# A gated attention block with a routed feed-forward part on one core: attention starts ahead of routing, normalized rows stay on chip, and value products are taken in plain fp32

## The reference

```python
# attn, per sequence (T=512, H=128, E=256, S=128)
xn2 = (xn - mean) / sqrt(var + EPS) * ln_w + ln_b
u, v, base = split(silu(xn2 @ uv_w.T + uv_b))
q, k = rope(base * gamma + beta)                 # two heads of one base
kernel = square(relu(q @ k.T / sqrt(S) + w[distance]))
attn = (u * (kernel @ v)) @ o_w.T + o_b + xn
# ffn, over all 4096 rows (8 experts, the best 2 of each row)
p = sigmoid(xn @ W_router); two largest, divided by their sum + 1e-6
ffn = sqrelu(xn @ W_sh_up) @ W_sh_down
    + sum over the two experts: weight * sqrelu(xn @ W_up[e]) @ W_down[e]
```

## Time and profile before

| | |
|---|---|
| median of 3 runs (lowest, highest) | 455.02 us (454.96, 456.42) |
| the profiled execution: its own time | 456.13 us |
| its span, first to last instruction | 454.3 us |
| PE busy | 371.5 us (82%), 2041 instructions |
| DVE busy | 294.0 us (65%), 726 |
| ACT busy | 245.2 us (54%), 453 |
| POOL busy | 176.2 us (39%), 159 |
| HBM read and written | 17.63 and 15.87 MB |
| mean granted TensorE clock | 0.927 of full |

### The profile page before, as it was taken

The page is one execution under the profiler, slowest core; times in us unless marked ns, Lnnn a source line. Parts: engine busy times, 40 slices in busy tenths (PEclk is TensorE's granted clock), DMA queues, the critical chain, the costliest instruction groups (busy, mean ns, idle before and its releaser), DMA issues.

```text
span 454.3 us, 8228 instructions
## 1 busy us (share of the span) xinstructions
PE 371.5 (82%) x2041; PEld 299.2 (66%) x2042; DVE 294.0 (65%) x726; ACT 245.2 (54%) x453; POOL 176.2 (39%) x159
## 2 busy tenths in 40 slices
PE   1168457799998989899999969999999999999800
PEld 1157435566665667566756638999999999999700
DVE  2889798988988888989899822333333333333245
ACT  0203027565676766665656715666666666666400
POOL 0486004562534526180716200444444444444500
PEclk9995567999999999999999997999999999999955
DMA  8618993000000001010100101221222212212089
GB/s 227 212 46 237 231 191 61 29 30 19 23 23 18 29 6 41 0 47 0 41 6 30 42 0 30 66 63 60 64 59 63 64 57 65 64 57 65 36 251 309
DMA packets 49792, 33.65 MB, mean 74 GB/s; under 512 B 5747, under 2 KB 46195, under 8 KB 49780
## 3 DMA queue, kind: packets, MB, share of 16 engines
q1 hardware_dynamic: 29120, 16.27, 12.8%
q10 hardware_dynamic: 16308, 8.26, 9.1%
q0 software_dynamic: 4352, 8.99, 5.5%
HBM read 17.63 MB, written 15.87 MB: 74 GB/s over the span
## 4 chain that ended last, share of the span: by engine, by line
PE 50%; DVE 21%; issue 12%; ACT 6%; ACTq 4%; DMA 4%; DVEq 2%; POOL 0%; POOLq 0%
PE bank L1133 14%; PE bank L1114 7%; PE bank L908 7%; PE bank L909 6%; PE bank L910 6%; DVE work L748 3%; PE bank L1020 3%; ACT base_qk L414 3%; DVE xs L613 3%; ACTq L356 2%; PE bank L946 2%; PE bank L1107 2%; DMA work<-results 2%; DVE qk_lo L725 2%; DVE k_lo L757 2%
## 5 line engine op out<-in xcount | busy, mean ns | idle before, releaser
L865 POOL DMA_INDIRECT slots_in<-xs,slot_now x64 | 75.2, 1176 | 124.5 <-DVE xs L634 77.9
L895 POOL DMA_INDIRECT results<-work x72 | 69.2, 960 | 109.2 <-DVE work L822 107.4
L822 DVE TENSOR_SCALAR work<-bank,work 128x128 f32<-128x128 f32 x72 | 25.2, 350 | 93.5 <-PE bank L1133 93.5
L1133 PEld LDWEIGHTS bank<-wdn,work 128*128 128x128 f32 x576 | 75.1, 191 | 6.0
L1133 PE MATMUL bank<-wdn,work 128*128 x576 | 75.7, 274 | 0.0
L499 ACT ACTIVATE work<-bank 128x512 f32<-128x512 f32 x72 | 43.1, 599 | 14.7 <-PE bank L1114 14.7
L505 ACT ACTIVATE work<-bank 128x512 f32<-128x512 f32 x72 | 43.1, 598 | 8.9 <-PE bank L910 3.4
L1114 PE MATMUL bank<-cst,work 128*128 128x128 f32 x288 | 43.9, 276 | 0.0
L908 PE MATMUL bank<-wup_lo,x_hi 128*128 x72 | 35.3, 491 | 1.0 <-DVE x_lo L813 1.0
L493 ACT CAST x_hi<-bank 128x128 fp32r<-128x128 f32 x72 | 19.0, 266 | 30.8 <-PE bank L1107 30.8
L1114 PEld LDWEIGHTS bank<-cst,work 128*128 128x128 f32 x288 | 34.2, 143 | 0.5 <-issue 0.4
(11 more groups left out here) (177 smaller groups left out, 824.1 us busy)
## 6 DMA issues: line engine op xcount, KB each, us to landing
slots_in<-spare ACTq DMA_DIRECT2D x1, 4680.0 KB, 31.7
work<-slots_in SPq DMA_DIRECT2D x36, 130.0 KB, 2.2
x_all<-in_L_attn_x SPq DMA_DIRECT2D x4, 512.0 KB, 8.7
work<-in_L_ffn_W_up SPq DMA_DIRECT2D x4, 512.0 KB, 3.5
wdn<-in_L_ffn_W_down SPq DMA_DIRECT2D x4, 512.0 KB, 7.3
work<-results SPq DMA_DIRECT2D x8, 256.0 KB, 7.2
work<-results ACTq DMA_DIRECT2D x8, 256.0 KB, 7.7
out<-x_all SPq DMA_DIRECT2D x8, 256.0 KB, 5.7
```

The costliest lines, as they stand in the source:

```text
L865: pool.indirect_dma_start(slots_in, bass.IndirectOffsetOnAxis(slot_now[:, k, t:t + 1], 0), xs1[:, k, t, :], None).then_inc(tokens_sent, 16)
L895: pool.indirect_dma_start(results, bass.IndirectOffsetOnAxis(dest[:, at:at + 1], 0), slot_y[:, k, :], None).then_inc(returned[k], 16)
L1133: last = pe.matmul(P_Y[h][:, 0:D], hid_t[:, h, rows], wdn[:, of, c, :].rearrange("p a d -> p (a d)"), start=(c == 0), stop=(c == HC - 1))
```

## The change

- The `Fori` loop over blocks is written out. Block 0 begins before routing; routing is cut in pieces that stand in blocks 0, 1 and 2.
- `x` comes in pieces of 4, 8, 10 and 10 tiles. Statistics and roots are taken for tiles 0 to 3 first, then for the other 28; the second norm's inverse is worked out on DVE (one more reciprocal), and both roots are asked for at once.
- `first_norm` writes normalized rows to `xs1` for all 32 tiles (132 wide: columns for a slot's address and weight on either side of the row). Groups 2 to 7 are made in block 0, and routing reads these same rows, turned by PE and copied by ACT. `second_norm` reads `xs1`.
- Each half row (130 of 132 columns, from column 0 or 2) is sent from `xs1` after the last routing piece; all 64 sends are one run on POOL. In the experts DVE adds the two column pairs of a slot row, since the pair that wasn't sent is zero.
- v and the squares are kept once, in fp32. `kernel_hi`, `kernel_lo`, `v_split` and one of two v silus are gone; `values` calls two plain matmuls instead of two `product`s.
- Weight casts go one expert at a time: in blocks 0 to 2 on ACT, their low halves and `add_rows` alternately on POOL. Down weights load after `routed`, since routing's scratch lies in their tile. The columns of gamma and beta, the cosines, the distance row and the zero fill move from ACT's queue to SP's.

The core of the diff (left out: names of semaphores, places of tiles, unchanged lines):

```diff
@@ sequence_turns @@
-            turn(0, True, False)
-            with eng.Fori(1, B - 1) as b:
-                turn(b, False, False)
-            turn(B - 1, False, True)
+            for b in range(B):
+                turn(b, b == 0, b == B - 1, b)
@@ ACT, turn @@
                 shared_square(b, 1)
+                if route == 0:
+                    routing_copied(2)
+                    routing_copied(3)
+                    routing_copied(4)
+                    routing_copied(5)
                 if not first:
                     output_out(b - 1)
-                kernel_hi(b, 0)
-                kernel_hi(b, 1)
+                if route == 1:
+                    weights_hi(3)
+                if route == 2:
+                    weights_hi(6)
                 shared_relu(b, 2)
                 shared_relu(b, 3)
+                if route == 0:
+                    routing_copied(6)
+                    routing_copied(7)
                 if not last:
                     second_rows_hi(b + 1)
                 shared_square(b, 2)
                 shared_square(b, 3)
-                kernel_hi(b, 2)
-                kernel_hi(b, 3)
+                if route == 0:
+                    weights_hi(1)
+                    weights_hi(2)
+                    routing_probs()
+                if route == 1:
+                    weights_hi(4)
+                    weights_hi(5)
+                if route == 2:
+                    weights_hi(7)
+                    weights_hi(8)
@@ DVE, routing's counts and statistics @@
+            def routing_counts():
+                dve.wait_ge(counted, 1)
+                dve.tensor_copy(place.rearrange(flat), banks[7][:, 0:NT * NE])
+                link(route_chain, dve.tensor_copy(sums[:, 0, 16:, :].rearrange(flat), banks[7][:, NT * NE:2 * NT * NE]))
+                dve.sem_inc(counts_kept, 1)
+                for n in range(5):
+                    src, dst, by = sums[:, n % 2], sums[:, (n + 1) % 2], 1 << n
...
+                link(stat_chain, dve.reciprocal(per_var[:, tiles], inv1[:, tiles]))
+                link(stat_chain, dve.tensor_tensor(inv2[:, tiles], var, per_var[:, tiles], ALU.mult))
+                dve.tensor_scalar(inv2[:, tiles], inv2[:, tiles], EPS, None, ALU.add).then_inc(var_made, 1)
@@ DVE, turn @@
                 qk_split(b)
+                if route == 0:
+                    first_norm(2)
+                    first_norm(3)
+                if route == 1:
+                    routing_first()
                 kernel_square(b, 0)
                 kernel_square(b, 1)
-                v_split(b)
+                if route == 0:
+                    first_norm(4)
+                    first_norm(5)
                 if not last:
                     second_norm(b + 1)
-                kernel_lo(b, 0)
-                kernel_lo(b, 1)
+                if route == 1:
+                    routing_second()
+                if route == 2:
+                    routing_counts()
                 kernel_square(b, 2)
                 kernel_square(b, 3)
+                if route == 0:
+                    first_norm(6)
+                    first_norm(7)
                 if not last:
                     second_rows_lo(b + 1)
-                    first_norm(b + 1)
+                if route == 1:
+                    routing_weights()
+                if route == 2:
+                    routing_tiles()
                 if not first:
                     mix(b - 1)
-                kernel_lo(b, 2)
-                kernel_lo(b, 3)
+                if route == 2:
+                    routing_slots()
                 if not last:
                     rotate_base(b + 1)
                     first_rows_lo(b + 1)
+                if route == 2:
+                    routing_owners()
@@ DVE, ahead of block 0 (the seven weight copies stand before this) @@
+            dve.wait_ge(inv_made, 1)
+            first_norm(0)
+            second_norm(0, True)
+            statistics(slice(FIRST, NT), ((1, (FIRST, 12)), (2, (12, 22)), (3, (22, NT))))
+            second_rows_lo(0)
...
+            dve.wait_ge(inv_made, 3)
+            first_norm(1)
             dve.wait_ge(ld["cos_sin"], 16)
-            first_norm(0, True)
             rotate_base(0)
             first_rows_lo(0)
@@ POOL @@
             pool.wait_ge(var_made, 1)
+            root(slice(0, 2), slice(0, FIRST))
+            pool.wait_ge(var_made, 2)
+            root(0, slice(FIRST, NT))
+            root(1, slice(FIRST, NT))
+            weights_lo(0)
+            for b in range(B):
+                add_rows(b)
+                weights_lo(b + 1)
+
+            pool.wait_ge(zero_filled, 16)
+            pool.wait_ge(slots_made, 1)
+            pool.sem_inc(sending, 1)
+            for t in range(NT):
                 for k in range(TOPK):
-                    pool.indirect_dma_start(slots_in, bass.IndirectOffsetOnAxis(slot_now[:, k, t:t + 1], 0),
-                                            xs1[:, k, t, :], None).then_inc(tokens_sent, 16)
+                    at = slice(k * 2, k * 2 + SENT_W)
+                    pool.indirect_dma_start(slots_in, bass.IndirectOffsetOnAxis(slot_i[:, k, t:t + 1], 0),
+                                            xs1[:, t, at], None, element_offset=k * 2).then_inc(tokens_sent, 16)
@@ PE, values and turn @@
-                    last = product(P_AV[e][:, :], v_hi[:, j, e * P:(e + 1) * P], v_lo[:, j, e * P:(e + 1) * P],
-                                   k_hi[:, j % 2, :], k_lo[:, j % 2, :], start=(j == 0), stop=(j == TB - 1))
+                    last = pe.matmul(P_AV[e][:, :], v[:, j, e * P:(e + 1) * P], kern[:, j, :], start=(j == 0), stop=(j == TB - 1))
...
                 uv_part("u1", b, P)
+                if route == 0:
+                    routing_logits(0)
+                    routing_logits(1)
+                if route == 2:
+                    routing_counted()
                 pe.wait_ge(qk_lo_made, START + b + 1)
                 scores(b, 0)
                 scores(b, 1)
+                if route == 0:
+                    routing_turned(2)
+                    routing_turned(3)
                 if not first:
                     output(b - 1)
                 scores(b, 2)
                 scores(b, 3)
+                if route == 0:
+                    routing_logits(2)
+                    routing_logits(3)
+                    routing_turned(4)
+                    routing_turned(5)
                 shared_up(b, 2)
                 shared_up(b, 3)
+                if route == 0:
+                    routing_logits(4)
+                    routing_logits(5)
+                    routing_turned(6)
+                    routing_turned(7)
                 pe.wait_ge(out_t_made, START + b)
                 shared_down(b, 0)
                 shared_down(b, 1)
+                if route == 0:
+                    routing_logits(6)
+                    routing_logits(7)
@@ PE, ahead of block 0 @@
             second_rows_turned(0)
+            uv_biases()
             base_part(0)
+            pe.wait_ge(ld["wr"], 16)
             first_rows_turned(0)
-            pe.wait_ge(routed, 1)
+            score_bias()
+            pe.wait_ge(bias_kept, 1)
+            routing_turned(0)
+            routing_turned(1)
```

549 lines of the change are left out of this document (253 added, 296 removed).

## The result

| | median, us | ratio to the kernel before, 95% interval |
|---|---|---|
| before | 455.25 (4 runs) | |
| changed | 451.77 (4 runs) | 0.9923 [0.9894, 0.9951] |
| forecast | 448.1 (range 437 to 458) | |

The change gains 3.5 us and not the 6.9 of the forecast: the direction and the range held, half the gain was missing. The profiled executions took 456.13 before (span 454.3) and 453.1 after (span 451.3).

What follows compares the result with a forecast made beforehand. It took each block to be bound by a loop through PE, ACT and DVE, not one engine's busy time. Terms -31.4, +27.7, -3.7 and +0.5 sum to -6.9 from the median 455.02, giving 448.1 us, range 437 to 458.

Steps and rivals of the forecast that it cites:

- The stretch ahead of block 0: Before block 0's rotation sum: the sum starts at 42.5 us instead of 73.9, -31.4 (bounds 39 and 47).
- Block 0: First block, now with the logits and turned groups: 41.1 us from its sum to the next (bounds 34.5 and 46).
- blocks 1 and 2: Blocks carrying routing pieces and POOL passes: 29 and 31.5 us (bounds 26 to 32 and 27 to 34).
- steady blocks: Blocks 3 to 6: 12.1 us scores to base plus 11.6 back, 23.7 instead of 24.64; -3.7 in all.
- The clock: Block 0: PE's first 3 to 5 us run at half speed after idling, +3 us.
- The last block: Last block, PE running from scores through values: 8 x 0.16 less 0.6 of wait for k_lo, given as +0.5 us.
- The sends: 64 sends in one piece from 136 us, 1.48 each, ending at 231, hidden; the last before 240.
- I cost it at nothing: Experts: one more 2-column DVE add per two tiles, a copy less, covered by DVE's wait for PE; 7 us without cover.
- Part 1: Value products: +1.3 us of PE a block, about 7.4 us off DVE a block; -0.9 a block.
- Routing riding free: Rival 1: hand-offs fall into gaps, blocks 0 to 2 cost 35, 26.5 and 28; 436 us; chance 0.18.
- Blocks gaining nothing: Rival 2: fp32 products eat what DVE gives back, blocks stay 24.64; 452 us; chance 0.12.
- POOL's passes: Rival 3: all 15 passes in blocks 0 to 2 hold DVE at 1.5 us each; +15, 463 us; chance 0.13.

Runs made afterwards that it cites:

- d1: Changed kernel with twelve unused floats behind zeros, moving work and slot_x by 32 bytes: 449.70 us, ratio 0.9891.
- e4: Kernel before with plain value products alone, plus one small VectorE copy per pair that delays the next slot load: 450.27 us, ratio 0.9888.
- g1: f4 with four semaphore increments added in VectorE's expert loop, in the even steps: 447.65 us, ratio 0.9855.
- g2: f4's instructions, with d1's edit of zeros in place of the shifted fetched results: 445.97 us, ratio 0.9803.
- d3: Changed kernel with the fetched results alone moved by eight floats (32 bytes) inside work: 448.90 us, ratio 0.9880.
- d2: Kernel before with w_sb 9 floats longer, so work and all behind it lie 32 bytes off: 457.45 us, ratio 1.0054.
- e3: d3 with value products as in the kernel before (three split fp32r products each): 458.64 us, ratio 1.0081.
- f4: e1 with VectorE's three small operations on a pair placed ahead of the scaling: 507.21 us, ratio 1.1135.
- e1: d3 with the next pair's slot load waiting for the pair's row sum, not its destinations: 448.30 us, ratio 0.9848.
- f1: Kernel before with plain value products alone, plus a VectorE copy in even expert steps that nothing waits for: 450.29 us, ratio 0.9909.
- f2: Kernel before with plain value products alone, plus e4's extra copy only in step 7 of each eight: 449.74 us, ratio 0.9873.
- f3: Kernel before with plain value products alone, plus e4's extra copy only in steps 1, 3 and 5: 451.25 us, ratio 0.9904.

## Why the prediction was wrong where it was

- **The stretch ahead of block 0** (42.5, measured 42.83): right, by its own steps: second root (to 37.2 for 36.7), wait, two rotations, one POOL pass and part of another.
- **Block 0** (41.1, measured 42.1), **blocks 1 and 2** (29 and 31.5, measured 27.7 and 30.3), **steady blocks** (23.7, measured 23.7; block 3 24.8): near, and right as to what bounds them. With the first sum they give 238.9 for the last one, measured 238.9. That it fits to the tenth is luck: 0.3 too little ahead of block 0, 1.5 too much in blocks 0 to 2 and 1.1 too little in block 3 cancel.
- **The clock** is the term in block 0 that was mis-sized: 3 to 5 us at 1.2 GHz for +3, measured 13.0 us. By d1 and the changed kernel (39.3 us with 5.3 at 1.2 GHz, 42.1 with 13.0) an us at 1.2 GHz costs 0.36, so these 13.0 cost some 4.7 us, by estimate. That is 1.7 more than forecast, and the block came 1.0 late, so its other terms were 0.7 too high together. Block 3 had 3.4 us at 1.2 GHz, from 144.6 to 148.0, behind two blocks in which TensorE was busy for 23.7 of 27.7 and 25.5 of 30.4 us; the forecast had none there.
- **The last block** (+0.5, measured +0.47 to the mix): its own terms, 8 x 0.16 less 0.6, give 0.7 and not 0.5, so this fit is luck too.
- **The sends** (last before 240): right, with 84.5/63 = 1.34 us a send where I took 1.48.
- **"I cost it at nothing"**, of the small operations in the experts: this step failed, and cost 2.2 us. It bounded their cost by VectorE's busy time and took as cover that VectorE waits for TensorE. The cover is there, but not where they stand: behind the scaling, ahead of the next x_lo, which TensorE's queue needs. Of the loss about 1.1 us is 0.11 to 0.18 at each of eight heads of the loop; the rest is mostly one step of 3.40 us, in which TensorE stood idle for 0.87 us until slot_x had come. e4 makes such a loss, g1 and g2 take it away. Why some 0.3 us of x_lo bites only at the head of the loop stays open: there TensorE's queue must also jump and read the next experts' numbers, but no run tells what that takes from it.
- **The end** stood in no term of the sum. It has the same bytes and instructions, so I took it as unchanged, without a reason for its rate; but the change moved `work` by a distance that is 32 bytes off a multiple of 512. Loss 2.3 us by the trace; moving the target alone gives 2.0 back in d3's and takes 2.8 in d2's. 448.1 + 2.2 + 2.3 less the 0.4 ahead of the first scaling and the 0.1 behind the last add is 452.1; measured 451.8.
- **Where the gain comes from**: Part 1 credited a steady block's gain to all 7.4 us that leave VectorE. A part of it is enough; behind that TensorE decides, and there the plain products cost 0.3 a block (23.72 against 23.43). Their worth is in blocks 0 to 2, 11 to 13.5 us, since VectorE is full of routing there; a part of it is the clock, which e3 had at 1.2 GHz for longer. I never worked out either half of the change alone.
- **Rivals.** Routing riding free: no, the first three blocks cost 26 us over plain ones. Blocks gaining nothing (452) had the right time for the wrong reason. POOL's passes: two operations of the first norm were caught, no square was.

## What to carry to other kernels

Put a price on where an added operation stands in its engine's queue, not on its length: move it into a wait of that engine, ahead of the operation that ends the wait. When a change resizes any buffer, compare the addresses of the tiles that transfers write, and the transfer rates of untouched stages, with those of before. When a stretch that wasn't edited takes another time, look first at its granted clock, and then at how long after a product its reader starts. Try each half of a double change alone: here one half had all the gain.

## What the runs showed of the hardware

- Fetches in 512-byte rows into SBUF ran at 345 to 346 GB/s in fifteen of the 20 kernels that were profiled, whose targets lie whole multiples of 512 bytes apart, and at 290 to 293 in the five whose targets lie 32 bytes below or above such a place, without exception.
- TensorE's clock stood at 1.2 GHz for 5.3 to 13.6 us of block 0 in kernels that differ elsewhere, and the same code took 39.3 to 42.4 us with it; block 3 took 24.6 to 26.2 with 3.4 or 6.9 us at 1.2 GHz.
- A kernel can lose 50 us through stalls in stages that an edit does not touch (f4, all runs), and win them back by four idle instructions or by other addresses. Signals of TensorE's products, on record 0.02 us behind their ends in e1, came up to 48 us behind them in f4, while those of ScalarE came at once. In small the same made steady blocks of f1, f2 and f3 take 24.3 to 25.1 us instead of 23.8.
- So two kernels' difference of 1 to 2 us is read from the stretch that was edited, not from the total alone.
